# Linear attention with scores on 32-row tiles, two heads at a time, in three pairs of PSUM banks

## The chip, the cores and the metric

The kernel runs on one core of a Trainium2 chip. The metric is the device time of one execution in microseconds. The whole program is a decoder of two layers; the change touches one stage of it, the linear attention near its beginning.

## The reference, cut to what matters

The input has 8 entries of 256 tokens with 128 features. The stage normalises them, projects them to q, k and v of 16 heads with 8 features each, and computes:

```
q, k = elu(x @ Wq) + 1, elu(x @ Wk) + 1          # all positive
# two chunks of 128 tokens, carried by S and z
scores = (q_c @ k_c.T) * tril(ones(128, 128))
num = q_c @ S + scores @ v_c ; den = q_c @ z + scores.sum(-1)
out = num / den + 1e-12
S += k_c.T @ v_c ; z += k_c.sum(0)
x = x + out @ Wo
```

The carried sums are the same as a causal product over all 256 tokens, and so the kernel computes it: a 256 by 256 score matrix per head in three blocks of 128 by 128, two on the diagonal (masked by a triangle) and a full one (keys of the first chunk, queries of the second).

## The kernel before, in words

Everything is fp32 and transposed: features lie on partitions, tokens on the free axis. `linear_attention_stage` works through the 8 entries; each engine has its own program, ordered by hand, and semaphores join them. TensorE runs strictly in the order written.

- `project` (L497, L500) multiplies a copy `xb` of the entry (made by ScalarE, L572) by the weights: q and k into bank 6, v into bank 7. ScalarE computes exp(min(x, 0)) in two steps (L577, L579) and copies v into a padded layout (L583). VectorE adds max(x, 0) (`features`, L613), forms the running sum of k (L616) and its product with q (L618).
- `denominator` (L509) sums that product over the features of a head into bank 4, and VectorE takes the reciprocal (L622).
- ScalarE makes `qm`: for each of the 16 heads a copy of q with all rows but the head's own 8 set to zero (L590).
- `score` (L518, L519): for one head, the full 128 rows of k against the full 128 rows of its `qm`, 256 columns for the first key chunk and 128 for the second, into bank 0 or 1 by turns. VectorE multiplies all three blocks by a mask whose middle block is ones (`keep_causal`, L628) into one of 8 slots of `sc`.
- `weigh` (L533): four heads at a time, v times the kept scores, each on its own 32 columns of the array, into bank 2 or 3.
- `divide` (L635, L637) and `out_projection` (L544, bank 5), and `finish` adds the result to x (L641).

Entries 2 to 5 run in a hardware loop, the others are written out. The steps of the next entry are put between the scores of this one. The next stage begins with the matmuls of its norm (L318).

Of the kernel before, what the change touches and what calls it, by code (L numbers as in the profile page):

```python
# [21 lines left out]
B = 8  # L22
# [391 lines left out]
def linear_attention_stage(c):  # L414
# [3 lines left out]

    nc = c.nc
    D = P // NH
    RS = 8
    GRP = 4
    NG = NH // GRP

    def head(n):

        return 4 * (n % 4) + n // 4

    with Stage(c, "la") as s:
        xb = s.sb("xb", [P, 2, L])
        low = s.sb("low", [P, 2 * L])
        qk = s.sb("qk", [P, 2, 2, L])
        qm = s.sb("qm", [P, 2, NH, L])
# [4 lines left out]
        sc = s.sb("sc", [P, RS, 3 * P])  # L444
        tri = s.sb("tri", [P, 3, P])
        ones = s.sb("ones", [P, L])
        mine = s.sb("mine", [P, NH])
        group = s.sb("group", [P, NH, D])
        on = s.sb("on", [P, L])
        (made, x_in, proj, v_proj, low_done, exp_done, feat, cum_done, qc_done, den_done, rec_done, v_done, qm_done,  # L450
         scores, sc_done, pv, scaled, on_done, out_done, x_done) = (s.sem(n) for n in (
            "made x_in proj v_proj low_done exp_done feat cum_done qc_done den_done rec_done v_done qm_done "
            "scores sc_done pv scaled on_done out_done x_done").split())

        def looped(eng, body):


            body(0, 0, True, True, False)
            body(1, 1, True, False, False)
            with eng.Fori(1, B // 2 - 1) as i:  # L460
                body(i * 2, 0, False, False, False)
                body(i * 2 + 1, 1, False, False, False)
            body(B - 2, 0, False, False, False)
            body(B - 1, 1, False, False, True)

        with nc.Block() as block:
            @block.gpsimd
            def _(pool):
                pool.memset(tri[:, :, :], 1.0).then_inc(made, 1)
                pool.memset(v[:, :, :, :, :], 0.0).then_inc(made, 1)  # L470
                pool.memset(mine[:, :], 1.0).then_inc(made, 1)
# [4 lines left out]
                for k in (0, 2):  # L476
                    pool.affine_select(out=tri[:, k, :], in_=tri[:, k, :], compare_op=ALU.is_ge, fill=0.0,
                                       base=0, pattern=[[1, P]], channel_multiplier=-1).then_inc(made, 1)

                for dst, rest in ((mine[:, :], []), (group[:, :, :], [[0, D]])):  # L480
                    pool.affine_select(out=dst, in_=dst, compare_op=ALU.is_ge, fill=0.0, base=0,
                                       pattern=[[-D, NH]] + rest, channel_multiplier=1).then_inc(made, 1)
                pool.wait_ge(made, 9)
                for dst, rest in ((mine[:, :], []), (group[:, :, :], [[0, D]])):
                    pool.affine_select(out=dst, in_=dst, compare_op=ALU.is_ge, fill=0.0, base=D - 1,
                                       pattern=[[D, NH]] + rest, channel_multiplier=-1).then_inc(made, 1)

            @block.tensor
            def _(pe):
                def project(b, p, first):  # L490

                    pe.wait_ge(x_in, b + 1)
                    if not first:
                        pe.wait_ge(feat, b)
                        pe.wait_ge(v_done, b)
                    for k in range(2):
                        mm = pe.matmul(c.ps[:, 6, k * L:(k + 1) * L], c.wqk[:, k, :], xb[:, p, :], start=True, stop=True)  # L497
                    mm.then_inc(proj, 1)
                    for t in range(2):
                        mm = pe.matmul(c.ps[:, 7, t * P:(t + 1) * P], xb[:, p, t * P:(t + 1) * P], c.wvo[:, 0, :],  # L500
                                       start=True, stop=True)
                    mm.then_inc(v_proj, 1)

                def denominator(b, first):

                    pe.wait_ge(qc_done, b + 1)
                    if not first:
                        pe.wait_ge(rec_done, b)
                    pe.matmul(c.ps[:, 4, 0:L], group[:, :, :].rearrange("p h d -> p (h d)"), qc[:, :],  # L509
                              start=True, stop=True).then_inc(den_done, 1)  # L510

                def score(b, p, n, first):
                    h = head(n)
                    bank = c.ps[:, n % 2, :]
                    pe.wait_ge(qm_done, b * NH + n + 1)
                    if n >= 2 or not first:
                        pe.wait_ge(sc_done, b * NH + n - 1)
                    pe.matmul(bank[:, 0:L], qk[:, p, 1, 0:P], qm[:, p, h, :], start=True, stop=True)  # L518
                    pe.matmul(bank[:, L:L + P], qk[:, p, 1, P:L], qm[:, p, h, P:L],  # L519
                              start=True, stop=True).then_inc(scores, 1)  # L520

                def weigh(b, p, g, fresh):

                    if g == 0:
                        pe.wait_ge(v_done, b + 1)
                        if not fresh:
                            pe.wait_ge(scaled, b - 1)
                    pe.wait_ge(sc_done, b * NH + (g + 1) * GRP)
                    for kt in range(2):
                        for n in range(g * GRP, (g + 1) * GRP):  # L530
                            h = head(n)
                            i, a = h // 4, h % 4
                            mm = pe.matmul(c.ps[32 * i:32 * i + 32, 2 + p, kt * P:L], v[:, p, kt, i, 32 * a:32 * a + 32],  # L533
                                           sc[:, n % RS, 0:L] if kt == 0 else sc[:, n % RS, L:L + P],
# [4 lines left out]
                def out_projection(b, fresh):  # L539

                    pe.wait_ge(on_done, b)
                    if not fresh:
                        pe.wait_ge(x_done, b - 1)
                    pe.matmul(c.ps[:, 5, 0:L], c.wvo[:, 1, :], on[:, :], start=True, stop=True).then_inc(out_done, 1)  # L544

                pe.wait_ge(made, 11)
                project(0, 0, True)
                denominator(0, True)

                def body(b, p, fresh, first, last):  # L550
                    for n in range(NH):
                        score(b, p, n, first)
                        if n == 1 and not first:
                            weigh(b - 1, 1 - p, NG - 1, True)
                        if n == 3 and not last:
                            project(b + 1, 1 - p, False)
                        if n == 6 and not first:
                            out_projection(b, fresh)
                        if n > GRP and n % GRP == 1:
                            weigh(b, p, n // GRP - 1, fresh)  # L560
                        if n == 12 and not last:
                            denominator(b + 1, False)
                looped(pe, body)
                weigh(B - 1, 1, NG - 1, True)
                out_projection(B, False)

            @block.scalar
            def _(act):
                def copy_x(b, p, fresh):
                    if not fresh:  # L570
                        act.wait_ge(v_proj, b - 1)
                    act.activation(xb[:, p, :], c.xn[:, ds(b * L, L)], ACT.Copy).then_inc(x_in, 1)  # L572

                def prepare(b, p, fresh):

                    act.wait_ge(proj, b + 1)
                    act.activation(low[:, :], c.ps[:, 6, :], ACT.Relu, scale=-1.0).then_inc(low_done, 1)  # L577
                    act.wait_ge(low_done, b + 1)
                    act.activation(low[:, :], low[:, :], ACT.Exp, scale=-1.0).then_inc(exp_done, 1)  # L579
                    act.wait_ge(v_proj, b + 1)  # L580
                    if not fresh:
                        act.wait_ge(pv, b * NG - NG)
                    act.activation(v[:, p, :, :, :].rearrange("p t i (a c) -> p (t i) a c", c=40)[:, :, :, 0:D],  # L583
                                   c.ps[:, 7, 0:L].rearrange("p (i a d) -> p i a d", a=4, d=D), ACT.Copy).then_inc(v_done, 1)
                    act.wait_ge(feat, b + 1)
                    if not fresh:
                        act.wait_ge(scores, b * NH - NH)
                    for n in range(NH):
                        h = head(n)
                        act.activation(qm[:, p, h, :], qk[:, p, 0, :], ACT.Copy, scale=mine[:, h:h + 1]).then_inc(qm_done, 1)  # L590

                act.wait_ge(made, 11)
                copy_x(0, 0, True)
                copy_x(1, 1, True)
                prepare(0, 0, True)

# [1468 lines left out]
```

## Time and profile before

| | us |
|---|---|
| median of three runs | 1999.63 (1999.55 to 2001.54) |
| the profiled execution | 2005.48, span 2003.7 |
| TensorE busy over the span | 1458.4 |
| VectorE busy | 1439.0 |
| ScalarE busy | 1154.3 |
| GpSimd busy | 1207.1 |

The stage of the change lies at 46 to 207 us of the span. The profile has the busy time of each engine (PE is TensorE's matmuls, PEld its weight loads, DVE VectorE, ACT ScalarE, POOL GpSimd), groups of equal instructions by line, and an order of time. [...]

### The profile page before, as it was taken

How to read it: one execution, taken by the hardware profiler on the slowest of the kernel's cores; microseconds unless marked ns; L12 is line 12 of the kernel's file. 1: busy time of each engine (PE TensorE's matmuls, PEld its weight loads, DVE VectorE, ACT ScalarE, POOL GpSimd, SP SyncE). 2: the span in 40 equal slices, each digit the busy share in tenths (PEclk: the TensorE clock that was granted, in tenths of full speed). 3: DMA queues.
4: the chain of work that ended last, by engine and by line, in shares of the span. 5: the costliest groups of instructions: out<-in, count | busy, mean ns of one | idle time of the engine just before them, and what ended most of it. 6: DMA issues, size and time to landing. Idle time of an engine off the chain costs nothing. (4 is left out here: it accounts for less than half of the span.)

```text
span 2003.7 us, 23749 instructions
## 1 busy us (share of the span) xinstructions
PE 1458.4 (73%) x6930; PEld 806.3 (40%) x6931; DVE 1439.0 (72%) x2510; ACT 1154.3 (58%) x2547; POOL 1207.1 (60%) x760
## 2 busy tenths in 40 slices
PE   3899899995654566565555665666346999999968
PEld 2777577773221112111111211212003677777623
DVE  3676488885419988998899988989982666566734
ACT  2543688875636555655455555555434777777720
POOL 1000356650039999999999999999991333333400
PEclk8999899996677777787677767777767999999978
DMA  3000000000044313342333323323303000000000
GB/s 100 1 1 1 1 2 1 0 1 0 11 159 169 150 67 125 148 170 112 141 149 148 120 93 149 148 106 147 148 0 84 1 1 2 1 0 1 1 0 21
DMA packets 51970, 134.40 MB, mean 67 GB/s; under 512 B 19076, under 2 KB 28568, under 8 KB 39448
## 3 DMA queue, kind: packets, MB, share of 16 engines
q1 hardware_dynamic: 49112, 130.78, 17.3%
q10 hardware_dynamic: 2496, 2.36, 0.4%
q8 instruction: 47, 0.77, 0.2%
q14 instruction: 59, 0.48, 0.1%
q0 software_dynamic: 256, 0.01, 0.0%
HBM read 114.26 MB, written 18.87 MB: 66 GB/s over the span
## 5 line engine op out<-in xcount | busy, mean ns | idle before, releaser
L1465 POOL TENSOR_TENSOR ma_hs<-ma_dtuR,ma_Bt 128x1024 f32<-128x1024 f32 x256 | 597.7, 2366 | 6.9 <-DMA ma_dtuR<-ma_dtu_d 6.6
L1624 ACT ACTIVATE ps<-ma_dtR,ma_A 128x512 f32<-128x512 f32 x512 | 332.7, 682 | 355.7 <-DVE ma_hs L1758 217.5
L788 POOL TENSOR_TENSOR x_pr<-x_pr,x_rec 128x512 f32<-128x512 f32 x256 | 267.2, 1044 | 341.3 <-DVE x_rec L1030 341.3
L1542 PE MATMUL ps<-ma_hs,ma_fold 128*32 128x512 f32 x1024 | 201.2, 927 | 285.6 <-POOL ma_hs L1473 229.5
L1752 DVE TENSOR_TENSOR_SCAN ps<-ps,ma_hs 128x1024 f32<-128x1024 f32 x144 | 329.1, 2286 | 6.0 <-POOL ma_hs L1465 4.1
L1752 DVE TENSOR_TENSOR_SCAN ma_hs<-ps,ma_hs 128x1024 f32<-128x1024 f32 x112 | 255.8, 2284 | 44.2 <-POOL ma_hs L1465 36.7
L996 ACT ACTIVATE x_pr<-x_sm,x_mx 128x256 f32<-128x256 f32 x512 | 254.6, 500 | 57.1 <-DVE x_mx L1021 51.3
L1473 POOL TENSOR_TENSOR ma_hs<-ma_hs,ma_Ct 128x1024 f32<-128x1024 f32 x112 | 264.4, 2362 | 0.0
L1542 PEld LDWEIGHTS ps<-ma_hs,ma_fold 128*32 128x32 f32 x1024 | 38.2, 146 | 416.2 <-issue 334.3
L1509 PE MATMUL ps<-ma_hn,ma_w_tap 128*128 128x512 f32 (+3 forms) x256 | 149.2, 749 | 59.5 <-ACT ma_hn L1642 47.8
L1758 DVE TENSOR_TENSOR ma_hs<-ps,ma_Ct 128x1024 f32<-128x1024 f32 x144 | 176.3, 1224 | 4.9
L1017 DVE TENSOR_TENSOR x_sm<-ps,x_m 128x512 f32<-128x512 f32 x128 | 87.7, 686 | 107.8 <-PE ps L840 106.5
L850 PE MATMUL ps<-ident,x_pr 128*128 128x128 f32 x1024 | 153.6, 273 | 0.9 <-DVE x_pT L922 0.4
L850 PEld LDWEIGHTS ps<-ident,x_pr 128*128 128x128 f32 x1024 | 127.0, 141 | 36.5 <-issue 13.6
L840 PE MATMUL ps<-x_k,x_q 128*128 128x256 f32 x512 | 138.3, 393 | 1.5 <-DVE x_sm L1017 1.5
L837 PE MATMUL ps<-x_km,x_q 128*128 128x256 f32 x512 | 136.2, 390 | 1.1 <-ACT x_km L966 1.0
L1021 DVE CUSTOM_DVE_ANT_0 x_sm<-ps,x_mr 128x256 f32<-128x256 f32 x256 | 97.5, 418 | 39.5 <-PE ps L837 38.3
L1509 PEld LDWEIGHTS ps<-ma_hn,ma_w_tap 128*128 128x128 f32 x256 | 60.8, 245 | 161.7 <-issue 161.7
L1021 DVE CUSTOM_DVE_ANT_0 x_sm<-x_sm,x_neg 128x256 f32<-128x256 f32 x256 | 103.5, 441 | 24.9 <-DVE x_sm L1017 24.9
L628 DVE TENSOR_TENSOR la_sc<-ps,la_tri 128x384 f32<-128x384 f32 x128 | 69.3, 551 | 46.5 <-PE ps L519 44.6
L840 PEld LDWEIGHTS ps<-x_k,x_q 128*128 128x128 f32 x512 | 87.1, 190 | 33.7 <-issue 20.5
L996 ACT ACTIVATION_READ_ACCUMULATOR x_pr<-x_sm,x_mx 128x1 f32 x512 | 97.3, 190 | 0.0
(309 smaller groups left out, 2472.3 us busy)
## 6 DMA issues: line engine op xcount, KB each, us to landing
ma_dtuR<-ma_dtu_d SPq DMA_DIRECT2D x32, 1024.0 KB, 7.1
ma_dtR<-ma_dt_d SPq DMA_DIRECT2D x32, 1024.0 KB, 8.9
ma_Bt<-ma_bc_d SPq DMA_DIRECT2D x16, 1024.0 KB, 5.0
ma_Ct<-ma_bc_d SPq DMA_DIRECT2D x16, 1024.0 KB, 6.9
ma_dtu_d<-ma_dtu SPq DMA_DIRECT2D x32, 256.0 KB, 2.0
ma_dt_d<-ma_dt SPq DMA_DIRECT2D x32, 256.0 KB, 2.3
ma_cwb<-in_L_attn_conv_w_dram SPq DMA_DIRECT2D x4, 512.0 KB
x_m<-in_mask_BxSxS_fk_dram SPq DMA_DIRECT2D x1, 2048.0 KB, 11.3
```

The source lines that it names most:

```text
L788: pool.tensor_tensor(pr[:, r, :, :], pr[:, r, :, :], rec[:, r, :].unsqueeze(2).broadcast_to([P, 2, L]), ALU.mult).then_inc(pr_done, 1)
L840: mm = pe.matmul(bank[:, t * L:(t + 1) * L], q[:, p, h // 2, t * P:(t + 1) * P], k[:, p, h, :], start=True, stop=True)
L850: mm = pe.transpose(c.ps[:, 2 + n % 2, kt * L + t * P:kt * L + (t + 1) * P], pr[:, n % RP, t, kt * P:(kt + 1) * P], c.ident[:, :])
L996: a = act.activation(pr[:, n % RP, t, :], sm[:, n % 2, t, :], ACT.Exp, bias=mx[:, n % 2, t:t + 1], scale=-1.0, accum_out=den[:, n % RP, t: ...
L1021: a = dve.tensor_tensor_reduce(sm[:, n % 2, t, :], bank[:, t, :] if small else sm[:, n % 2, t, :], mr[:, p, :] if small else neg[:, t, :], ...
L1465: pool.tensor_tensor(hs[:, k % SLOTS, :, :], dtuR[:, unit(f, h), q, :].unsqueeze(1).broadcast_to([P, 2, CH]), rows(Bt, k), ALU.mult).then_ ...
L1473: pool.tensor_tensor(hs[:, k % SLOTS, :, :], hs[:, k % SLOTS, :, :], rows(Ct, k), ALU.mult).then_inc(c_pool, 1)
L1509: mm = pe.matmul(out, w_tap[:, b, TAPS - 1 - e, h * P:(h + 1) * P], src, start=(e == 0), stop=(e == TAPS - 1), skip_group_check=True)
L1542: mm = pe.matmul(c.ps[q * E32:(q + 1) * E32, Y[h], :], fold[:, :], hs[:, (k0 + q) % SLOTS, a, :], start=False, stop=(j % 2 == 1 and a == 1 ...
L1624: e = act.activation(c.ps[:, 2 * (k % 2) + a, :], dtR[:, unit(f, h), q, :], ACT.Exp, scale=A[:, (f // QUARTERS) % 2, h, q, no:no + 1])
L1752: dve.tensor_tensor_scan(out, pair(k), slot(k), 0.0, ALU.mult, ALU.add).then_inc(scan_done, 1)
L1758: dve.tensor_tensor(hs[:, k % SLOTS, :, :], c.ps[:, 2 * (k % 2):2 * (k % 2) + 2, :], rows(Ct, k), ALU.mult).then_inc(c_vector, 1)
```

## The change

- A score now uses only the 32 rows on which its head lies. `qm` has 4 copies instead of 16: copy a keeps head a of each group of four, so that one copy serves four heads, each in its own 32 rows. Its mask `member` is summed by VectorE from `mine`.
- `score` works on two heads (a pair) at once, on two 32-row tiles of the array, each into its own bank; three pairs of banks (0 to 5) go round. Eight pairs are an entry.
- `keep_causal` (VectorE) masks only the diagonal blocks of a pair in one operation; `keep_full` (ScalarE) copies the full blocks, after VectorE. `sc` has 16 slots.
- Bank 6 holds the weighted sums, and bank 7 (`W`) serves projection, values, denominator and output projection in turn, each behind waits for the one before. `project_values` is a step of its own and waits for `features`; `denominator` waits for `v_done`; `out_projection` waits for the reciprocal of two entries later (`min(b + 3, B)`).
- The copy `xb` is gone; the product `qc` and the addition of 1e-12 move to GpSimd. All loops are written out.

The diff, cut to its core (the old lines stand in the code above; setting up of masks is left out):

```diff
-    RS = 8
+    RS = 16
+    NPAIR = NH // 2
+        PV, W = 6, 7
+        def banks(j):
+            return slice(2 * (j % 3), 2 * (j % 3) + 2)
+        def slots(j):
+            return slice(2 * (j % NPAIR), 2 * (j % NPAIR) + 2)
...
+                def weighted_q(b):
+                    pool.wait_ge(cum_done, b + 1)
+                    if b >= 1:
+                        pool.wait_ge(den_done, b)
+                    pool.tensor_tensor(qc[:, :], qk[:, b % 2, 0, :], cum[:, :], ALU.mult).then_inc(qc_done, 1)
+                def add_eps(b):
+                    pool.wait_ge(scaled, b + 1)
+                    pool.tensor_scalar(on[:, :], on[:, :], 1e-12, None, ALU.add).then_inc(on_done, 1)
...
+                def project(b):
+                    if b >= 1:
+                        pe.wait_ge(v_done, b)
+                        pe.wait_ge(rec_done, b)
+                    if b >= 3:
+                        pe.wait_ge(x_done, b - 2)
...
+                def project_values(b):
+                    pe.wait_ge(feat, b + 1)
...
+                def denominator(b):
                     pe.wait_ge(qc_done, b + 1)
+                    pe.wait_ge(v_done, b + 1)
...
+                def score(b, m):
+                    j = b * NPAIR + m
+                    a, p = m // 2, b % 2
+                    pe.wait_ge(qm_done, 4 * b + a + 1)
+                    if j >= 3:
+                        pe.wait_ge(sc_act, j - 2)
+                    for kt in range(2):
+                        for r in range(2):
+                            i = 2 * (m % 2) + r
+                            row = slice(32 * i, 32 * i + 32)
+                            mm = pe.matmul(c.ps[:, 2 * (j % 3) + r, 2 * kt * P:2 * P + kt * P],
+                                           qk[row, p, 1, kt * P:(kt + 1) * P], qm[row, p, a, kt * P:L], start=True, stop=True)
+                    mm.then_inc(scores, 1)
+                def weigh(b, g):
...
+                    pe.wait_ge(sc_dve, b * NPAIR + 2 * g + 2)
+                    pe.wait_ge(sc_act, b * NPAIR + 2 * g + 2)
...
+                def out_projection(b):
+                    pe.wait_ge(on_done, b + 1)
+                    pe.wait_ge(v_done, min(b + 3, B))
+                    pe.wait_ge(rec_done, min(b + 3, B))
+                    if b >= 1:
+                        pe.wait_ge(x_done, b)
...
+                for b in range(B):
+                    for m in range(NPAIR):
+                        score(b, m)
+                        if m == 0 and b >= 1:
+                            weigh(b - 1, NG - 1)
+                        if m == 1 and b + 1 < B:
+                            project(b + 1)
+                        if m == 3 and b + 1 < B:
+                            project_values(b + 1)
+                        if m in (3, 5, 7):
+                            weigh(b, m // 2 - 1)
+                        if m == 4 and b + 1 < B:
+                            denominator(b + 1)
+                        if m == 6 and b >= 1:
+                            out_projection(b - 1)
...
+                def keep_full(b, m):
+                    j = b * NPAIR + m
+                    act.wait_ge(sc_dve, j + 1)
+                    if j >= NPAIR:
+                        act.wait_ge(pv, (j - NPAIR) // 2 + 1)
+                    act.activation(sc[:, slots(j), 1, :], c.ps[:, banks(j), P:2 * P], ACT.Copy).then_inc(sc_act, 1)
...
+                for b in range(B):
+                    for m in range(NPAIR):
+                        keep_full(b, m)
+                        if b + 1 < B:
+                            if m == 1:
+                                exponentials(b + 1)
+                            if m >= 4:
+                                own_rows(b + 1, m - 4)
+                            if m == 4:
+                                values(b + 1)
...
+                def keep_causal(b, m):
...
+                    dve.tensor_tensor(sc[:, slots(j), 0:3:2, :],
+                                      c.ps[:, banks(j), 0:3 * P].rearrange("p r (a q) -> p r a q", a=3)[:, :, 0:3:2, :],
+                                      tri[:, :].unsqueeze(1).unsqueeze(1).broadcast_to([P, 2, 2, P]), ALU.mult).then_inc(sc_dve, 1)
...
+                for b in range(B):
+                    for m in range(NPAIR):
+                        keep_causal(b, m)
+                        if m == 2 and b >= 1:
+                            divide(b - 1)
+                        if m == 2 and b + 1 < B:
+                            features(b + 1)
+                        if m == 5 and b + 1 < B:
+                            invert(b + 1)
+                        if m == 7 and b >= 1:
                             finish(b - 1)
```

## Rows read from the trace of the kernel before

**Rows 1.** Groups of instructions, 0 to 330 us: line, engine, operation, shapes, count | busy, mean ns | idle before
```profile
L518 PE MATMUL ps<-la_qm,la_qk 128*128 128x256 f32 x256 | 82.7, 405 | 8.3 <-DVE la_sc L628 5.6 <-ACT la_qm L590 1.7
L628 DVE TENSOR_TENSOR la_sc<-ps,la_tri 128x384 f32<-128x384 f32 x128 | 69.3, 551 | 46.5 <-PE ps L519 44.6
...
L590 ACT ACTIVATE la_qm<-la_qk,la_mine 128x256 f32<-128x256 f32 x128 | 51.9, 494 | 35.2 <-DVE la_qk L613 35.2
...
L622 DVE RECIPROCAL la_rec<-ps 128x256 f32<-128x256 f32 x8 | 14.0, 1749 | 0.8 <-PE ps L509 0.8
...
L613 DVE SCALAR_TENSOR_TENSOR la_qk<-ps,la_low 128x512 f32<-128x512 f32 x8 | 5.5, 682 | 9.1 <-ACT la_low L579 9.1
...
L579 ACT ACTIVATE la_low<-la_low 128x512 f32<-128x512 f32 x8 | 5.0, 629 | 0.3
...
L577 ACT ACTIVATE la_low<-ps 128x512 f32<-128x512 f32 x8 | 4.8, 597 | 33.1 <-PE ps L497 33.1
...
L635 DVE TENSOR_TENSOR la_on<-ps,la_rec 128x256 f32<-128x256 f32 x8 | 3.3, 415 | 1.0 <-PE ps L533 1.0
...
L583 ACT ACTIVATE la_v<-ps 128x256 f32<-128x256 f32 x8 | 2.9, 366 | 0.0
```

**Rows 2.** Order of time, the additions of `finish`: start us, us, engine, line
```profile
104.58 0.41 DVE L641 TENSOR_TENSOR xT<-xT,ps 128x256 f32 x1
...
195.97 0.41 DVE L641 TENSOR_TENSOR xT<-xT,ps 128x256 f32<-128x256 f32 x1
...
206.43 0.42 DVE L641 TENSOR_TENSOR xT<-xT,ps 128x256 f32<-128x256 f32 x1 [0.79 <-PE ps L544]
```

**Rows 3.** Busy us (count) in a stretch: PE, PEld, DVE, ACT, POOL, granted clock, DMA, GB/s
```profile
86.00:194.00 108.00, 101.27 (x824) 80.21 (x823) 74.97 (x137) 47.97 (x116) 0.00 (x0) 1.00 0.00 1
```

**Rows 4.** Order of time, PE, a score at either clock
```profile
58.49 1.06 PE L518 MATMUL ps<-la_qm,la_qk 128*128 128x256 f32 x2
59.35 0.63 PE L519 MATMUL ps<-la_qm,la_qk 128*128 128x128 f32 x2
...
71.80 0.60 PE L518 MATMUL ps<-la_qm,la_qk 128*128 128x256 f32 x2
...
72.46 0.38 PE L509 MATMUL ps<-la_qc,la_group 128*128 128x256 f32 x1
```

**Rows 5.** Order of time, PE, a `weigh` and the score behind it
```profile
110.41 0.86 PE L533 MATMUL ps<-la_sc,la_v 128*32 128x256 f32 x16
...
111.20 0.30 PEld L518 LDWEIGHTS ps<-la_qm,la_qk 128*128 128x128 f32 x2 [0.20 <-ACT la_qm L590]
```

**Rows 6.** Busy times and granted clock of seven stretches, columns as in rows 3
```profile
57.90:61.20 3.30, 3.23 (x11) 2.52 (x10) 2.56 (x3) 3.30 (x9) 0.00 (x0) 0.50 0.00 0
61.30:64.70 3.40, 3.40 (x22) 3.06 (x21) 1.62 (x3) 2.48 (x6) 0.00 (x0) 1.00 0.00 0
...
484.50:522.00 37.50, 28.73 (x141) 13.29 (x141) 30.78 (x87) 27.16 (x51) 0.00 (x0) 0.50 0.00 0
...
1952.20:1955.60 3.40, 3.40 (x6) 0.93 (x5) 1.22 (x1) 0.00 (x0) 0.00 (x0) 0.50 0.00 0
1955.60:1959.00 3.40, 3.40 (x6) 0.54 (x5) 0.01 (x1) 0.00 (x0) 0.00 (x0) 0.50 0.00 0
1959.10:1962.40 3.30, 3.30 (x4) 1.02 (x4) 1.18 (x1) 0.00 (x0) 0.00 (x0) 0.50 0.00 0
1962.60:1976.00 13.40, 13.40 (x35) 4.42 (x35) 6.62 (x6) 0.00 (x0) 0.00 (x0) 1.00 0.00 0
```

**Rows 7.** GpSimd: a group over the whole span, and the end of its set-up
```profile
L788 POOL TENSOR_TENSOR x_pr<-x_pr,x_rec 128x512 f32<-128x512 f32 x256 | 267.2, 1044 | 341.3 <-DVE x_rec L1030 341.3
...
50.62 0.40 POOL L485 TENSOR_SCALAR_AFFINE_SELECT la_group<-la_group 128x128 f32<-128x128 f32 x1
```

**Rows 8.** Order of time, PE, eight-row matmuls between full ones
```profile
1953.32 1.03 PE L1863 MATMUL ps<-moe_pTb,moe_sel 8*128 8x512 bf16 x2
...
1957.99 1.03 PE L1863 MATMUL ps<-moe_pTb,moe_sel 8*128 8x512 bf16 x2
```

More of the change, by code:

```diff
@@ L474, in _ @@
                 pool.wait_ge(made, 5)
[L476 to L480, printed above, removed]
+                pool.affine_select(out=tri[:, :], in_=tri[:, :], compare_op=ALU.is_ge, fill=0.0,
+                                   base=0, pattern=[[1, P]], channel_multiplier=-1).then_inc(made, 1)
@@ L510, in denominator @@
                               start=True, stop=True).then_inc(den_done, 1)
[L512 to L520, printed above, removed]
@@ L529, in weigh @@
                     for kt in range(2):
[L530 to L534, printed above, removed]
+                        for i in range(4):
+                            n = g * GRP + i
+                            mm = pe.matmul(c.ps[32 * i:32 * i + 32, PV, kt * P:L],
+                                           v[:, p, kt, i, 32 * g:32 * g + 32],
+                                           sc[:, n % RS, 0:2, :].rearrange("p a q -> p (a q)") if kt == 0 else sc[:, n % RS, 2, :],
@@ L537, in weigh @@
                     mm.then_inc(pv, 1)
[L539 to L562, printed above, removed]
@@ new lines, in _ @@
+                pe.wait_ge(made, 10)
+                project(0)
+                project_values(0)
+                denominator(0)
+                for b in range(B):
[13 more added lines that the diff above has]
+                            out_projection(b - 1)
@@ L567, in _, with exponentials @@
+                weigh(B - 1, NG - 1)
+                out_projection(B - 1)
             @block.scalar
             def _(act):
[L569 to L574, printed above, removed]
+                def exponentials(b):
                     act.wait_ge(proj, b + 1)
-                    act.activation(low[:, :], c.ps[:, 6, :], ACT.Relu, scale=-1.0).then_inc(low_done, 1)
+                    if b >= 1:
+                        act.wait_ge(feat, b)
+                    act.activation(low[:, :], c.ps[:, W, :], ACT.Relu, scale=-1.0).then_inc(low_done, 1)
@@ L578, in prepare, with values @@
                     act.wait_ge(low_done, b + 1)
                     act.activation(low[:, :], low[:, :], ACT.Exp, scale=-1.0).then_inc(exp_done, 1)
+                def values(b):
                     act.wait_ge(v_proj, b + 1)
[L581 to L584, printed above, removed]
@@ L585, in prepare @@
-                    act.wait_ge(feat, b + 1)
[L586 to L595, printed above, removed]
-                prepare(1, 1, True)
@@ L599, in _ @@
-                copy_x(2, 0, False)
-                prepare(2, 0, False)
-                copy_x(3, 1, False)
-                with act.Fori(1, B // 2 - 1) as i:
-                    for p in range(2):
-                        prepare(i * 2 + p + 1, 1 - p, False)
-                        copy_x(i * 2 + p + 2, p, False)
-                prepare(B - 1, 1, False)
+                    if b >= 2:
+                        act.wait_ge(pv, (b - 1) * NG)
+                    act.activation(v[:, b % 2, :, :, :].rearrange("p t i (a c) -> p (t i) a c", c=40)[:, :, :, 0:D],
+                                   c.ps[:, W, 0:L].rearrange("p (i a d) -> p i a d", a=4, d=D), ACT.Copy).then_inc(v_done, 1)
@@ new lines, in _ @@
+                exponentials(0)
+                act.wait_ge(member_done, 1)
+                act.wait_ge(made, 10)
+                for a in range(4):
+                    own_rows(0, a)
+                values(0)
+                for b in range(B):
+                    for m in range(NPAIR):
+                        keep_full(b, m)
+                        if b + 1 < B:
+                            if m == 1:
[4 more added lines that the diff above has]
+                                values(b + 1)
@@ L639, in finish @@
                 def finish(b):
                     dve.wait_ge(out_done, b + 1)
-                    dve.tensor_tensor(c.xT[:, ds(b * L, L)], c.xT[:, ds(b * L, L)], c.ps[:, 5, 0:L],
-                                      ALU.add).then_inc(x_done, 1)
-                dve.wait_ge(made, 11)
-                features(0, 0)
-                invert(0, 0)
-                def body(b, p, fresh, first, last):
-                    for n in range(NH):
-                        keep_causal(b, n, first)
-                        if n == 2 and not first:
-                            divide(b - 1, 1 - p)
-                        if n == 7 and not first:
-                            finish(b - 1)
-                        if n == 8 and not last:
-                            features(b + 1, 1 - p)
-                        if n == 13 and not last:
-                            invert(b + 1, 1 - p)
@@ L659, in _ @@
-                looped(dve, body)
-                divide(B - 1, 1)
+                    dve.tensor_tensor(c.xT[:, tokens(b)], c.xT[:, tokens(b)], c.ps[:, W, 0:L], ALU.add).then_inc(x_done, 1)
+                dve.wait_ge(made, 10)
+                dve.tensor_reduce(member[:, :], mine[:, :, :], AX.X, ALU.add).then_inc(member_done, 1)
+                features(0)
+                invert(0)
+                for b in range(B):
+                    for m in range(NPAIR):
[7 more added lines that the diff above has]
+                        if m == 7 and b >= 1:
+                            finish(b - 1)
@@ L661, in _ @@
+                divide(B - 1)
                 finish(B - 1)
```

112 lines of the change are left out of this document (54 added, 58 removed).

## The prediction

> **What bounds the kernel now.** I read the groups of instructions of the stage first, then the busy times by stretch, then the order of time over a few entries of the batch, then the granted clock. The stage is eight alike entries; `finish` (L641) of entries 1 and 6 begins at 104.58 and 195.97 [rows 2], five entries apart, so one entry takes (195.97 - 104.58)/5 = 18.28 us. In 86 to 194 us PE is busy 101.27 of 108 us at granted clock 1.00, DVE 74.97 and ACT 47.97 [rows 3]: PE is the bound. Its largest part is the 16 scores of an entry, 256 wide and 256 narrow passes in all, each fp32 matmul being two passes; the wide ones stand in [rows 1]. DVE idles 46.5 us before its mask multiply, nearly all of it for PE [rows 1], so DVE's saving alone is worth nothing.
>
> A score back to back at 2.4 GHz runs from 71.80 to 72.46, 0.65 us; I use 0.64 (wide passes 0.213 apart, narrow ones 0.107). At 1.2 GHz the two wide passes take 59.35 - 58.49 = 0.86 us and the narrow ones 0.43, so 1.28 [rows 4]. One `weigh` is 16 passes from 110.41; with its four column groups side by side it streams the same 0.64, and the next score starts at 111.20, 0.79 later, with 0.20 of PE idle ahead of it [rows 5]. So I charge 0.12 us for each change between kinds of tile.
>
> **The change, part by part.** Names: S0 to S7 are the eight new pair scores of an entry, W0 to W3 its `weigh`s, K and F what VectorE and ScalarE do to a pair.
> - PE. A pair is 8 passes on two 32-row tiles in two banks. If the two tiles run side by side, a pair streams what a single head did: 0.64 at 2.4 GHz, 1.28 at 1.2. That removes 8 x 0.64 = 5.1 us an entry. No row of before has row tiles side by side. The bounds are 0.64 (as column tiles do in [rows 5]) and 1.28 (one after the other); I take 0.64, since the two tiles also write different banks.
> [...]
> - DVE. K: 8 x 512 elements instead of 16 x 384. No row has this four-part pattern; 512 elements from PSUM take 0.682 (L613), so 5.5 against 8.8 us [rows 1]. The bounds are 0.68 and twice that; 0.68 taken. `qc` goes to POOL, so does the epsilon.
> - ACT. 16 row copies become 4 (0.41 us apart in a run, x128 in 51.9 us [rows 1]), plus eight F of 256 elements, as L583, 0.37. Some 6.5 us an entry, hidden except where named below. The copies of x (L572) go.
> - POOL. `qc` lies between half of L788 and all of it, 0.5 to 1.04 us [rows 7], and its result is wanted over 4 us later: nothing. The epsilon, as wide, is hidden but in the last entry (0.9 us of the same bounds).
> - Loops unrolled: PE idles 6.7 of 108 us in all [rows 3], so the turns of the loop cost less than that; more code to load shows in no row. 0 taken, bounds -1 and +2 us.
> - One bank (W = 7) now serves projection, values, denominator and output, so these go one after another, and PE, in order, holds the next scores behind each. That is the new path.
>
> The path of an entry, from the end of S7's stream. A: W2, S0, W3, S1, `project`, S2 on PE, then 0.2 until DVE starts. B: K2 0.68, `divide` 0.42, `features` 0.68 and gaps, 2.0 (the two exponentials, 0.60 + 0.63, end before the divide does); `project_values` waits for it, and W0 and S4 behind it. C: these three and 0.2. D: K4 0.68, F4, `own_rows`, `values`, 1.93 with gaps: `denominator` waits for `v_done`, S5 behind it. E: denominator, S5, 0.2. G: K5 0.68 and the reciprocal 1.75, 2.48: `out_projection` waits for `rec_done`, S7 behind it. H: out, S7.
>
> At 2.4 GHz: A 5 x 0.64 + 0.85 + 6 x 0.12 + 0.2 = 4.97; B 2.0; C 0.43 + 1.28 + 0.36 + 0.2 = 2.27; D 1.93; E 0.43 + 0.64 + 0.24 + 0.2 = 1.51; G 2.48; H 0.43 + 0.64 + 0.24 = 1.31. Sum 16.5 us, against 18.28.
> At 1.2 GHz: A 6.4 + 1.71 + 0.72 + 0.25 = 9.08; B 2.0; C 0.85 + 2.56 + 0.36 + 0.25 = 4.02; D 1.93; E and G together 0.85 + 1.28 + 0.24 + 2.8 = 5.17 (W1 and S6 now last as long as the reciprocal); H 0.85 + 1.28 + 0.24 = 2.37. Sum 24.6 us.
>
> **The clock.** This decides the sign. In the new order PE streams only some 9.7 of 16.5 us at 2.4 GHz, with waits of 1.9 to 2.5 us, and a pair uses 64 of 128 rows. What rows say: with full-height matmuls and 94% busy the clock keeps 1.00 [rows 3]. At 57.9 to 61.2, busy 3.23 of 3.3 us with full scores, it is 0.50, and then 1.00. But in 484.5 to 522 it is busy 28.73 of 37.5 us and stays at 0.50 for all of it. And in 1952.2 to 1959 it is busy 6.8 of 6.8 us and stays at 0.50, where 8-row matmuls (L1863, 1.03 us each time) stand between full ones; 1959.1 to 1962.4, which is L1870 alone, has 0.50 too, and then it is 1.00 [rows 6, 8]. So full business is not enough where part of it is on few rows. The new stage starts at 1.2 GHz, as the old one (first score at 58, [rows 4]), but has a pair on half the rows where the old one had full ones, and waits. I expect it to stay at 1.2 GHz nearly throughout. [...]
>
> **The sum.** POOL's set-up ends at 51.0 [rows 7]; one select and two thirds of a memset fewer, and no copy of x, bring the first projection 1 us forward, and `values` behind four row copies and `denominator` behind it take that back: first score at 57.7, as now. Entry 0 lacks W3 and out: 24.6 - 1.5 - 1.0 = 22.1. Entries 1 to 6: 147.6. Entry 7 has no preparation: 8 x 1.28 + 3 x 1.28 + 0.85 + 8 x 0.12 = 15.9. Tail: K7, F7, W3, divide, epsilon, out, finish: 6.2. End at 57.7 + 22.1 + 147.6 + 15.9 + 6.2 = 249.5, against 206.43 + 0.42 = 206.85 [rows 2]: 42.6 us later. Nothing behind changes but the clock with which the norm begins, +-2. On the profiled execution (2005.48, span 2003.7) that is 2048; the median of the runs lies 5.85 below that execution, so 2042.
>
> **The rivals.**
> - Back at 2.4 GHz: two tiles side by side count as a full array, so the dense stretch A raises the clock each time and only the waits of D and G lower it. For it: the rise after 61.2 [rows 6], and that PE kept 1.00 with 6.7 of 108 us idle [rows 3]. Against: the other rows of [rows 6, 8]. All fast: 57.7 + 14.9 + 6 x 16.5 + 8.4 + 4.2 = 184.2, 22.6 early, 1977. A quarter of the time slow adds 2 us an entry: 200.8, 6 early, 1994. I price it 1987. It is on the other side, and the point from which it decides is the mean path of an entry falling below about 19 us, which is 70% of its time at 2.4 GHz.
> - The tiles don't run side by side, so the change doesn't do what it says: seven of the eight S on the path grow by their own length. At 1.2 GHz 9 us an entry more, 69 in all: 2111. At 2.4 GHz an entry is 20 us (part of S3 and S6 fills waits): 215, 8 late, 2008. For: no row shows row tiles side by side. Against: column tiles do it, 16 passes in 0.86 us [rows 5].
> - DVE's and ACT's relief is hidden anyway, and PE's gain is eaten exactly by the waits: within 4 us.
>
> **How the numbers follow.** Stuck at 1.2 GHz with tiles side by side 0.55 (own range 2028 to 2054: some fast stretches, or 0.2 more for a pair); back at 2.4 GHz 0.28; tiles one after another 0.12, a third of it at the slow clock; the rest 0.05. A measurement of this kernel tells some 0.2% (4 us) from no change. Faster: 0.28 x nearly all + a little, 0.30; within 0.2% 0.05; slower 0.65. The range leaves out the all-fast end below 1978 and the slow serial case above 2058.
>
> **What would show it.** Granted clock of 60 to 240 us: about 0.5 (right) or above 0.8 (first rival). Pair: the starts of the two tiles' passes some 10 ns apart and eight passes in 1.28 us at 1.2 GHz, or 2.5. `finish` 24.6 us apart. PE idle before L500's successor for `features`, before the denominator for `values`, before the output for the reciprocal; each 1 to 2.5 us. K near 0.68. If `finish` is under 18 us apart, the step on the clock is what failed.

## The result and the profile after

The changed kernel takes 2037.87 us (median of four runs, 2031.78 to 2044.84) against 1999.89 before: the ratio is 1.019, with a 95% interval of 1.0167 to 1.0213. It is slower by 38 us; the forecast was 2042. Its profiled execution is the slowest of the four, 2044.84 us, span 2043.1.

The stage ends with the last L665 (242.11 us); before it ended at 206.85 [rows 2]. That is 35.3 of the 39.4 us between the two spans. The next stages add the rest in small pieces: the norm right behind (L318) starts 35.3 us later than before, the one of L377 38.1 us (569.7 against 531.6), and the L318 of the second layer 39.4 us (1566.11 against 1526.75).

The groups of the stage after, in 98.9 to 225.3 us (five entries); columns as in [rows 1], which they answer:

```profile
L527 PE MATMUL ps<-la_qm,la_qk 32*128 32x256 f32 x160 | 42.1, 698 | 0.0
...
L651 DVE TENSOR_TENSOR la_sc<-ps,la_tri 128x512 f32<-128x512 f32 x40 | 27.5, 689 | 81.1 <-PE ps L527 81.1
...
L600 ACT ACTIVATE la_qm<-la_qk,la_member 128x256 f32<-128x256 f32 x20 | 10.0, 499 | 0.0
...
L514 PE MATMUL ps<-la_qc,la_group 128*128 128x256 f32 x10 | 5.4, 642 | 9.9 <-ACT la_v L593 9.9
...
L507 PE MATMUL ps<-wvo,xn 128*128 128x128 f32 x20 | 5.1, 397 | 8.5 <-DVE la_qk L635 8.5
```

DVE's new mask operation costs 0.69 us where 0.68 was charged, and saves what was said: 5.5 against 8.8 us an entry. It buys nothing, for DVE now waits 81.1 us in five entries for the scores. PE's two new waits stand in the last two rows: 9.9/5 = 2.0 us an entry for `values` before the denominator, and 8.5/5 = 1.7 for `features` before the values.

Why the scores are late stands in the busy times by entry, from one `finish` to the next (columns as in [rows 3]):

```profile
98.46:123.01 24.55, 20.89 (x144) 12.97 (x140) 9.03 (x14) 6.15 (x15) 1.58 (x2) 0.57 0.00 1
123.01:147.75 24.74, 21.06 (x144) 13.16 (x140) 9.04 (x14) 6.15 (x15) 1.58 (x2) 0.57 0.00 1
147.75:172.66 24.91, 21.24 (x144) 13.22 (x140) 9.04 (x14) 6.14 (x15) 1.57 (x2) 0.57 0.00 1
172.66:198.82 26.16, 22.42 (x144) 13.85 (x140) 9.04 (x14) 6.22 (x15) 1.57 (x2) 0.50 0.00 1
...
225.00:241.00 16.00, 13.05 (x159) 8.66 (x152) 6.65 (x12) 3.85 (x10) 1.70 (x2) 0.82 0.00 1
```

An entry takes 24.6 to 26.2 us, the granted clock is 0.50 to 0.57, and PE is busy 85% of the time at that clock. Before, it was 18.28 us at 1.00 [rows 2, 3]. The traces give a granted clock and no frequency; what the prediction and the expectations call 1.2 and 2.4 GHz are the granted clocks 0.50 and 1.00. Two wide passes of a score take 0.86 us at 0.50 [rows 4] and 0.44 at 1.00 (71.80 to 72.24 in `before`). Over 86 to 142 us of the changed kernel, read in steps of 0.1 us, 490 of the 560 steps have 0.50, 66 have 1.00 and the four others lie where it changed; so a value between, like the 0.57, is a mean over both. The last entry has no preparation and so neither of the two waits; there the clock comes up near 230.5 us and the mean is 0.82.

The clock also came up inside three of these entries, for a short time. In the entry shown further down it was 0.50 although PE had worked without a break since 113.8 us. It was 1.00 from 131.5 to 134.9, and then 0.50 again:

```profile
113.85:131.40 17.55, 17.55 (x108) 10.77 (x112) 5.45 (x7) 4.04 (x10) 0.00 (x0) 0.50 0.00 1
131.50:134.90 3.40, 1.69 (x32) 1.06 (x24) 2.90 (x5) 0.67 (x3) 1.47 (x2) 1.00 0.00 0
137.00:143.00 6.00, 4.43 (x28) 2.57 (x30) 1.95 (x3) 1.83 (x5) 0.00 (x0) 0.50 0.01 3
```

PE stood still for half of the fast stretch, because it waited for `features` until 133.52. So the fast clock came when there was least to do with it.

One entry in order of time (start us, us, engine, line; left out are the weight loads and the other engines):

```profile
120.70 1.65 PE L527 MATMUL ps<-la_qm,la_qk 32*128 32x256 f32 x8
122.28 1.51 PE L542 MATMUL ps<-la_sc,la_v 128*32 128x256 f32 x16
...
123.72 1.65 PE L527 MATMUL ps<-la_qm,la_qk 32*128 32x256 f32 x8
...
128.32 2.08 PE L501 MATMUL ps<-xn,wqk 128*128 128x256 f32 x4
...
130.33 1.48 PE L527 MATMUL ps<-la_qm,la_qk 32*128 32x256 f32 x16
...
131.84 0.69 DVE L651 TENSOR_TENSOR la_sc<-ps,la_tri 128x512 f32<-128x512 f32 x1 [2.71 <-PE ps L527]
...
133.52 0.71 PE L507 MATMUL ps<-wvo,xn 128*128 128x128 f32 x4 [1.71 <-DVE la_qk L635]
...
136.65 0.69 DVE L651 TENSOR_TENSOR la_sc<-ps,la_tri 128x512 f32<-128x512 f32 x1 [1.87 <-PE ps L527]
...
138.57 1.19 PE L514 MATMUL ps<-la_qc,la_group 128*128 128x256 f32 x2 [1.97 <-ACT la_v L593]
139.69 1.36 PEld L527 LDWEIGHTS ps<-la_qm,la_qk 32*128 32x128 f32 x8 [0.65 <-issue]
...
144.29 1.22 PE L555 MATMUL ps<-la_on,wvo 128*128 128x256 f32 x2
```

A pair is one row of 8 passes: each of its four matmuls stands as two instructions (the 256-wide ones of L527 are x160 for the 80 heads of five entries). The next operation starts 1.58 us later (120.70 to 122.28), of which 1.28 is taken to be streaming at the clock of 0.50; by the same estimate one tile after the other would take 2.56. At 130.33 two pairs, S2 and S3, stand in one row: their 16 passes on four different row tiles ran together in 1.48 us, with nothing between them (the clock rose just before their end).

### The profile page after: what moved, and what is told of

Its sections match the earlier page's. It is cut to its first block and busy times, and to the rows that moved or that the text cites. A ratio compares the mean times of both kernels' runs of the same rounds, so it can differ in the third digit from the quotient of the medians.

```text
span 2043.1 us, 23493 instructions
## 1 busy us (share of the span) xinstructions
PE 1477.5 (72%) x6931; PEld 793.5 (39%) x6931; DVE 1410.1 (69%) x2431; ACT 1137.2 (56%) x2507; POOL 1219.3 (60%) x775
## 5 line engine op out<-in xcount | busy, mean ns | idle before, releaser
L1018 ACT ACTIVATE x_pr<-x_sm,x_mx 128x256 f32<-128x256 f32 x512 | 254.6, 500 | 57.7 <-DVE x_mx L1043 52.6
L1564 PEld LDWEIGHTS ps<-ma_hs,ma_fold 128*32 128x32 f32 x1024 | 38.1, 145 | 417.2 <-issue 335.0
L651 DVE TENSOR_TENSOR la_sc<-ps,la_tri 128x512 f32<-128x512 f32 x64 | 43.6, 687 | 110.8 <-PE ps L527 110.8
L482 POOL TENSOR_SCALAR la_on<-la_on 128x256 f32<-128x256 f32 x8 | 6.8, 851 | 161.1 <-DVE la_on L661 161.1
```

Source lines behind the costliest of these rows:

```text
L1018: a = act.activation(pr[:, n % RP, t, :], sm[:, n % 2, t, :], ACT.Exp, bias=mx[:, n % 2, t:t + 1], scale=-1.0, accum_out=den[:, n % RP, t: ...
L1564: mm = pe.matmul(c.ps[q * E32:(q + 1) * E32, Y[h], :], fold[:, :], hs[:, (k0 + q) % SLOTS, a, :], start=False, stop=(j % 2 == 1 and a == 1 ...
```

## The experiments

Each kernel was timed beside the kernel before on the same chip, where that took 1999.9 to 2003.4 us, and the ratio is to it. "Entry" is the distance of two `finish` in the middle of the stage, "clock" the granted clock over 86 to 142 us; both are of one profiled execution.

| kernel | us | ratio, 95% | entry | PE busy of 56 | clock |
|---|---|---|---|---|---|
| before | | | 18.4 | 52.8 | 1.00 |
| changed | 2037.9 | 1.019 (1.0167 to 1.0213) | 24.6 to 26.2 | 46.7 | 0.56 |
| before_32rows | 2064.4 | 1.0316 (1.0295 to 1.0337) | 24.2 to 27.9 | 52.4 | 0.56 |
| after_fullrows | 2019.6 | 1.0078 (1.0051 to 1.0106) | 20 to 21.6 | 50.2 | 0.91 |
| after_filled | 1993.5 | 0.9941 (0.992 to 0.9963) | 16.9 | 55.9 | 1.00 |
| after_quads | 1981.1 | 0.9888 (0.9869 to 0.9907) | 17.1 | 45.0 | 0.71 |
| after_quads_filled | 1969.5 | 0.9852 (0.9819 to 0.9884) | 14.2 | 55.8 | 1.00 |
| after_split_banks | 1964.5 | 0.9815 (0.9778 to 0.9852) | 13.1 | 53.2 | 1.00 |
| after_reordered | 1960.0 | 0.9797 (0.9768 to 0.9827) | 12.5 | 50.3 | 1.00 |
| after_quads_reordered | 1952.0 | 0.9765 (0.9731 to 0.9799) | 11.4 | 47.1 | 1.00 |
| after_filled_32rows | 2037.3 | 1.0203 (1.015 to 1.0257) | 24 | 55.1 | 0.56 |
| after_warm_start | 2042.6 | 1.0212 (1.0173 to 1.0251) | 23.3 to 26.2 | 47.7 | 0.56 |
| after_again | 2044.0 | 1.0218 (1.0181 to 1.0256) | 24.7 to 26.2 | 48.7 | 0.56 |

**1. Only the rows, in the kernel before.** No instruction more or less, no bank or wait changed:

```diff
-                    pe.matmul(bank[:, 0:L], qk[:, p, 1, 0:P], qm[:, p, h, :], start=True, stop=True)
+                    row = slice(32 * (h // 4), 32 * (h // 4) + 32)
+                    pe.matmul(bank[:, 0:L], qk[row, p, 1, 0:P], qm[row, p, h, :], start=True, stop=True)
```

> The kernel before with one thing changed: each score matmul reads only the 32 rows on which its head lies; number, width and order of all instructions stay. Theory (few rows keep the clock low): the granted clock of 86 to 194 us falls from 1.00 to about 0.5 although PE stays over 85% busy, an entry goes from 18.3 to 24 to 30 us, and the kernel to 2045 to 2095 us. Rival (only waits lower the clock): PE has as few waits as before, so the clock stays near 1.00 and the kernel lies within 10 us of 2000, or below it if neighbouring tiles overlap.

Measured: 61 us slower. Its busy times:

```profile
86.00:194.00 108.00, 101.09 (x572) 68.20 (x568) 50.57 (x93) 33.17 (x80) 0.00 (x0) 0.56 0.00 1
```

PE is busy 101.09 of 108 us, as good as the 101.27 of [rows 3], and the clock is 0.56 in place of 1.00. So 32-row matmuls, one tile at a time, take the clock away without any wait more than before. For this kernel the rival is out.

**2. Full rows in the changed kernel.**

```diff
-                            row = slice(32 * i, 32 * i + 32)
+                            row = slice(0, P)
```

> The changed kernel with its score matmuls over all 128 rows (what it leaves out: the scores of the four heads of a group are summed and not kept apart). Order, waits, banks and the work of DVE and ACT stay; the two heads of a pair can't run side by side. Theory (few rows keep the clock low): granted clock of the stage 0.9 or more, a pair 1.28 us, an entry about 20 us, the kernel 2005 to 2020, so faster than the changed kernel although PE does twice the score work. Rival (waits keep the clock low): clock 0.6 or less, a pair 2.56 us, an entry over 30 us, the kernel above 2090.

Measured: 2019.6. PE does twice the score work in the same order, and the kernel is 18 us faster than the changed one, because the clock stays at 0.91 to 1.00:

```profile
86.00:194.00 108.00, 94.30 (x729) 74.47 (x730) 46.39 (x67) 31.60 (x79) 7.92 (x10) 0.95 0.00 1
```

The waits are not all the same, though. The one for `values` is still 2.0 us, but the longer scores fill most of the one for `features` (three entries, 95.04 to 157.73 us: in total, times, longest):

```profile
PE ps L514 <- ACT la_v L593: 5.9, 3, 2.0
PE ps L507 <- DVE la_qk L635: 1.2, 3, 0.4
```

A pair takes 1.50 us at a clock of 1.00 here, the change of tile included (95.11 to 96.61), and 0.85 on 32 rows (107.30 to 108.15 in `after_filled`). PE idles 13.7 of 108 us here and 16.7 in the changed kernel. So full-height work kept most of the clock behind a wait of 2.0 us an entry. What it would keep behind 1.7 and 2.0 us together, this run does not show.

**3. Useless work in the waits.** Ten matmuls an entry, four before `project_values`, four before `denominator`, two before `out_projection`; each writes the bank that the next pair overwrites:

```diff
+                def fill(j, n):
+                    if j >= 3:
+                        pe.wait_ge(sc_act, j - 2)
+                    for _ in range(n):
+                        pe.matmul(c.ps[:, 2 * (j % 3), 0:L], c.centre[:, :], c.xn[:, 0:L], start=True, stop=True)
```

> The changed kernel with ten useless full-height matmuls of 256 columns an entry ahead of the three waits (four before the values, four before the denominator, two before the output). Theory (few rows and waits together keep the clock low): the fill lies in waits of 1.7 to 2.3 us, the clock rises to 0.75 or more, an entry falls below 22 us and the kernel below 2025. Rival (the clock in this stage doesn't answer to full-height work in the waits): it stays at 0.5 to 0.6, 8.5 us of fill at 1.2 GHz overrun the waits by 2 to 4 us, and the kernel is at 2050 to 2070.

Measured: 1993.5. Added work makes the changed kernel 44 us faster, and faster than the kernel before; an entry is 16.9 us, near the 16.5 forecast for the high clock. One stretch of it:

```profile
110.85 0.95 PE L527 MATMUL ps<-la_qm,la_qk 32*128 32x256 f32 x16
111.73 1.99 PE L535 MATMUL ps<-xn,centre 128*128 128x256 f32 x8
...
115.78 1.99 PE L535 MATMUL ps<-xn,centre 128*128 128x256 f32 x8
117.82 0.67 PE L514 MATMUL ps<-la_qc,la_group 128*128 128x256 f32 x2
```

The fill (L535) takes up the wait for `features` and nearly all of that for `values`; two pairs take 0.95 us where they took 1.48 in the change, most of it at a granted clock of 0.50.

**4. The same fill on 32 rows.** This asks whether it is the rows of the fill that help, or that PE is busy:

```diff
-                        pe.matmul(..., c.centre[:, :], c.xn[:, 0:L], ...)
+                        pe.matmul(..., c.centre[64 * (j % 2):64 * (j % 2) + 32, :], c.xn[64 * (j % 2):64 * (j % 2) + 32, 0:L], ...)
```

> The filled kernel (1993 us, clock 1.00) with the same ten fill matmuls an entry, as many columns, at the same places, but on 32 rows instead of 128. Theory (rows count, so such fill is nearly idle time to the clock): clock 0.5 to 0.65, an entry 25 to 29 us and the kernel 2035 to 2070. Rival (any matmul in the waits keeps the clock, whatever its rows): clock 0.95 or more and 1988 to 1998 us.

Measured: 2037.3, a ratio of 1.020 like that of the changed kernel (1.019 and 1.022). Its four executions scatter widely, 2024.9 to 2052.9, and the profiled one is the fastest. There the first distance of two `finish` is 28.3 us and the others are 24.0, a little under the 25 to 29 expected. Here are two rows, the first of the full fill, the second of the 32-row one:

```profile
86.00:142.00 56.00, 55.86 (x538) 39.13 (x530) 30.19 (x44) 20.62 (x51) 4.76 (x6) 1.00 0.00 1
```
```profile
86.00:142.00 56.00, 55.12 (x351) 34.66 (x350) 21.11 (x29) 13.15 (x33) 3.15 (x4) 0.56 0.00 1
```

PE is busy 100% and 98% of the time, and the clock is 1.00 and 0.56. The rows that the fill uses are all that was edited. Two things follow from that edit: a part of the 32-row fill runs beside the pair on other rows (its passes of 107.65, 108.24 and 108.66 us start between those of the pair that begins at 107.62), and a wait for `values` of up to 0.9 us an entry is left.

**5. Four tiles at once.** Scores of both pairs of a group are issued together, and wait for one pair of banks more (`sc_act >= j - 1`):

```diff
+                    if m % 2:
+                        return
...
+                        for i in range(4):
```

> The changed kernel with the two pairs of four heads issued as one, so that all four 32-row tiles run side by side and all 128 rows are in use; it waits for one pair of banks more. Theory (rows in use are what counts): the clock in the scores is that of full-height work, 0.8 or more over the stage; four heads stream in 0.64 us, an entry takes 15 to 18 us and the kernel 1980 to 2005. Rival (a row tile counts little whatever its neighbours do, or the waits decide): clock 0.5 to 0.6, an entry 21 to 23 us, the kernel 2015 to 2035.

Measured: 1981.1, entry 17.1, so the time fell where the theory put it; but the clock missed its forecast, 0.71 against "0.8 or more". The two waits are those of the changed kernel (four entries, columns as in experiment 2), and PE is busy 45.01 of 56 us:

```profile
PE ps L514 <- ACT la_v L595: 7.9, 4, 2.0
PE ps L507 <- DVE la_qk L637: 6.8, 4, 1.7
```

So even four tiles at once do not keep the clock at 1.00 behind these waits: 0.71, where pairs have 0.56. Two things gained time, all 128 rows in use and half as many score steps on the path; their shares were not separated. The profiled execution is also the slowest of five, 10 us above the median. That the waits hold the clock down here, the same fill as in experiment 3 shows:

> The four-tile scores with ten useless full-height matmuls an entry ahead of the same three waits. Quads alone gave 1981 at a clock of 0.67 to 0.84. Theory (what is left of the low clock is the waits): clock 0.95 or more, the fill of 4.3 us lies inside the waits, 1965 to 1978. Rival (the fill is as long as what the clock gives back): 1978 to 1990.

Measured: 1969.5, entry 14.2, clock 1.00.

**6. The waits without the fill.** In `after_split_banks` q and k, values with output, and denominators have a bank each and the pairs have two pairs of banks; in `after_reordered` the banks are as in the change and only the order differs:

```diff
-                        if m == 3 and b + 1 < B:
+                        if m == 4 and b + 1 < B:
                             project_values(b + 1)
+                        if m == 7 and b + 1 < B:
+                            denominator(b + 1)
...
-                        if m == 4 and b + 1 < B:
-                            denominator(b + 1)
-                        if m == 6 and b >= 1:
+                        if m == 5 and b >= 1:
                             out_projection(b - 1)
```

On DVE `finish` moves to m == 5 and `invert` to m == 7; `denominator` also waits for `x_done`, and `out_projection` for the reciprocal of one entry earlier than in the change.

> The changed kernel with the one shared bank undone: q and k, values with output, and denominators have a bank each, and the pairs of heads go round two pairs of banks instead of three. The waits for features, values and reciprocal on PE go. It tells apart the two things that keep the clock low. If few rows alone are enough: PE is busy over 85% at a granted clock of 0.5 to 0.7, an entry takes 19 to 22 us (PE's own work at 1.2 GHz is some 21.8) and the kernel 2005 to 2025. If the waits were what kept it low: clock 0.9 or more, an entry 13 to 15 us, the kernel 1955 to 1980.

> The changed kernel, pairs as they are, with the steps that share the bank put later in PE's order, so that each finds its wait over: values after the fifth score, output after the sixth, denominator after the eighth, reciprocal last on DVE. Waits of 2 us no longer lie on PE, rows are as in the change. If few rows alone keep the clock low: 0.5 to 0.7, an entry 19 to 22 us, the kernel 2000 to 2025. If the waits did: clock 0.9 or more, 1950 to 1975.

Measured: 1964.5 and 1960.0, both at clock 1.00 with pairs on half the rows as in the change. Both came out as forecast for the case that the waits did it: for pairs, few rows alone are not enough to lose the clock. The longest wait of PE that is left is 0.4 us in the first and 1.2 us in the second. Together with the other experiments the theory has to be narrower. One tile of 32 rows at a time loses the clock at 94% busy. Two tiles at a time lose it only with the waits of 1.7 and 2.0 us, and four tiles with the same waits lose a part of it.

The clock over time, read in steps of 0.1 us, adds what tells these cases apart: how soon it comes back. With full rows (after_fullrows) it fell at 108.6 us, behind the wait for `values`, and was back at 112.1. With four tiles (after_quads) it fell at 112.0, behind the wait for `features`, and was back at 122.3. In the change it fell at 111.0, behind the same wait, and was back only at 131.5, although PE was busy for all of the last 17.55 us before that. Counted from the end of the last wait (107.82, 116.67 and 113.83 us) it was back after 4.3, 5.6 and 17.7 us. So the clock fell behind a wait in all three, and with fewer rows in use it came back later.

> The same later order with the two pairs of four heads issued as one. Rows in use and no waits on PE: clock 0.95 or more, PE's own work some 8.7 us an entry and DVE's 9.4, so DVE or the three pairs of banks set 10 to 13 us an entry, and the kernel is at 1940 to 1968. Rival (the bank chain, not the clock, sets the entry): 14 us or more, 1970 to 1990.

Measured: 1952.0, the fastest, 48 us below the kernel before. An entry is 11.4 us, of which PE is busy 39.24/4 = 9.8 and DVE 34.59/4 = 8.6; neither is full, and what sets the 11.4 was not looked into:

```profile
89.42:135.03 45.61, 39.24 (x564) 26.14 (x565) 34.59 (x53) 23.35 (x60) 6.30 (x8) 1.00 0.01 2
```

**7. A fast start.** Sixteen fill matmuls ahead of the first score and none later.

> The changed kernel with sixteen useless full-height matmuls ahead of its first score only, so that the stage starts at 2.4 GHz. Theory (the waits of every entry bring the clock down again, and pairs on half the rows don't bring it back): the first entry is some 6 us shorter, the clock is at 0.6 or less from the second entry on, the kernel 2028 to 2042. Rival (the stage has two lasting states and the low start chooses the slow one): clock above 0.85 throughout, an entry 16 to 18 us, the kernel 1978 to 1995.

Measured: 2042.6, just above the forecast and no better than the changed kernel beside it (2044.0). Its clock:

```profile
58.00:80.00 22.00, 17.70 (x186) 13.08 (x188) 11.18 (x14) 6.84 (x18) 0.73 (x1) 1.00 0.01 1
80.00:100.00 20.00, 16.34 (x126) 9.81 (x120) 8.34 (x12) 5.35 (x14) 1.61 (x2) 0.59 0.00 1
```

The first entry ran at a granted clock of 1.00, its waits of 1.5 and 2.0 us included, and took 12.0 us from its first score where the changed kernel took 19.0; the clock fell near 84 us, behind the next wait for `features`, in the second entry. So the low clock is the order's own, not handed on from the low start that I had pointed to.

> The changed kernel itself once more, beside the two others on their chip, to have its entries and its clock from a second execution. Both theories: 2030 to 2045 us, entries of 24 to 26.5 us.

Measured: 2044.0, entries 24.74, 24.91, 26.09, 26.16, 24.70.

## Why the prediction was right, point by point

- **The clock step** was the one that decided, and it held: 0.57 over 60 to 240 us and 0.50 to 0.57 by entry, against "about 0.5". That full business is not enough where part of it is on few rows, as read from [rows 6, 8], is borne out by experiments 1 and 4; the stretch of those rows itself was not tested. What the prediction had too simple is the share of the waits: half the rows alone do not do it (after_reordered, 1.00), and the waits alone were only tested with four tiles at once (after_quads, 0.71) or in part (after_fullrows, 0.91 to 1.00). PE busy 98% at 0.56 (`after_filled_32rows`) and 100% at 1.00 (`after_filled`) differ in the rows of the fill, so the measurement decides against busy time as the only measure.
- **Terms that no run shows.** No trace has the 1.2 and 2.4 GHz by which the sums are named: what was measured is a granted clock of 0.50 and of 1.00, and two wide passes in 0.86 us at the one and 0.44 at the other. Nor does a run show the 0.2 us more for a pair that the range allows for: a pair and the change of tile behind it took 1.58 us at 0.50 (120.70 to 122.28) and 0.85 at 1.00 (107.30 to 108.15 in `after_filled`), where 1.40 and 0.76 were charged.
- **The path of an entry** was put at 24.6 us for the low clock; measured 24.55, 24.74, 24.91, and 26.1 in two entries that had no stretch at 1.00. Parts measured between 122.1 (the end of S7's stream, 120.70 + 1.43) and 146.9: A 9.7 (9.08 forecast), B 1.7 (2.0), C 3.1 (4.02), D 1.9 (1.93), E and G 5.7 (5.17), H 2.6 (2.37). The changes of tile were mis-sized: at 0.50 a pair and a `weigh` together take 3.02 us (120.70 to 123.72) for 2.56 of streaming, so 0.23 for a change, not 0.12. In B and C a stretch at 1.00 (131.5 to 134.9 us) gave this back; in the entries without one it shows as the 26.1. So the 24.6 was hit partly by luck: for 0.50 throughout the sum is 1.5 us short.
- **The reciprocal**: at 0.50 W1 and S6 last as long, as said; the output at 144.29 waits for nothing of DVE.
- **Side by side**: right, and more than said. Pairs with nothing between them overlapped too (16 passes in 1.48 us at 130.33); S3 was not on the path, so this changed no sum. At a clock of 1.00 the next operation starts 0.85 us behind a pair (107.30 to 108.15 in after_filled) and 0.87 behind four tiles (89.31 to 90.18 in after_quads_reordered), the change of tile included; so the 0.64 for the stream of a pair alone was not measured by itself.
- **DVE, ACT, POOL**: 0.69 for K against 0.68; POOL's `qc` 0.73 and the epsilon 0.85, inside their bounds, and hidden but for the epsilon of the last entry, as said.
- **The stage's end** was put at 249.5 and came at 242.1. The first score began at 56.94, not 57.7. So the stage lasted 185.2 us where 191.8 were forecast. The last entry ran at a clock of 0.82 and ended 12.66 us after the one before it (`finish` at 224.91 and 237.57), where the prediction had the whole stage at the low clock.
- **The total is nearer than its parts, and that is luck.** Against the forecast, the start was 0.8 us early, the first two entries were 6.1 us short (40.6 against 46.7), the next five 3.5 us long (126.45 between their `finish` against 123.0), and the last entry with its tail 4.0 us short (18.1 against 22.1). The stages behind added 4.1 us where 0 with bounds of 2 was taken. In sum the profiled execution came 3 us under its 2048, and the median 4 us under 2042.
- **The rival on the other side** (back at the high clock, 1977 to 1994) is what `after_filled` shows: 1993.5. Its sum of a path of 16.5 us was nearly right, 16.9 measured. In the change itself its mechanism was there but weak: the dense stretch A did raise the clock in some entries, only at its end (at 131.5 us, 17.7 us behind the last wait), and one wait later it was down again.
- **Unrolling**: no run has the change with the loop kept, so its 0 stands untested.

## What to carry to other kernels

Row tiles side by side saved array time (four heads in 0.88 us, 110.85 to 111.73 in `after_filled`, where one head took 0.66 on full rows, 71.80 to 72.46 [rows 4]), but few rows also cost the clock (61 us in before_32rows). Before cutting a matmul to 32 rows, ask what else fills the other rows meanwhile, and issue as many tiles side by side as the banks allow. A wait on TensorE cost more than its length where the clock fell behind it (0.56 in the change, 1.00 in `after_reordered`), so put each step that needs another engine's answer so late that the answer is there; here the order alone was worth 78 us. When a gain in work turns into a loss, compare the granted clock of the stretch first; a fill of useless full-height matmuls is a quick test, not a cure.

## What the runs showed of the hardware

- At like busy shares of PE (86 to 142 us) the granted clock differed. At 94% busy it was 1.00 for full rows (before) and 0.56 for 32-row tiles one at a time (before_32rows). At 98 to 100% it was 1.00 with a fill on 128 rows and 0.56 with one on 32. At 83 and 84% it was 0.56 for pairs with waits of 1.7 and 2.0 us an entry (the change) and 1.00 for four tiles with no wait over 1.2 us (after_quads_reordered).
- Pairs with no wait over 1.2 us: 1.00, at 90 and 95% busy. Four tiles with waits of 1.7 and 2.0 us: 0.71. Full rows with waits of 2.0 and 0.4 us: 0.91 to 1.00.
- The way back to a granted clock of 1.00, from the end of the last wait to the rise of the clock: 4.3 us with full rows (after_fullrows, back at 112.1), 5.6 with four tiles (after_quads, 122.3), 17.7 with pairs (the change, 131.5).
- More work took less time: the fill of `after_filled`, an estimated 4.3 us an entry (20 passes that start 0.215 us apart, 112.05 to 112.48), took 7.8 us off it.
- The low state does not come from the start: in `after_warm_start` the granted clock was 1.00 over 58 to 80 us, 0.59 over 80 to 100 and 0.50 over 84 to 88, in the second entry.
- Row tiles of successive instructions ran together where no wait and no other kind of tile stood between: 16 passes on four tiles in 1.67 us at 0.50 (119.23 in after_quads) and 0.94 at 1.00 (89.31 in after_quads_reordered), against 1.65 (120.70 in the change) and 0.92 (107.30 in after_filled) for the 8 of a pair.
- A change between row tiles and column tiles cost, by an estimate that takes 1.28 us of streaming each at 0.50 and 0.64 at 1.00, some 0.23 us at 0.50 (3.02 us for 2.56 of streaming, two changes). At 1.00 a pair and a `weigh` back to back take 1.64 us (107.30 to 108.94 in after_filled) for 1.28, 0.18 each.
- How rows in use and waits add up to the granted clock was not measured beyond these cases.
